# Layer 1 of a two-layer graph attention kernel: ten score products and seven own-slot products as a few wide VectorE instructions

## The chip, the cores and the metric

The kernel runs on one core of one Trainium2 chip. The metric is device time of one execution in microseconds (us). Before the change it is 2040.26 us, the median of three runs (2037.29 to 2045.88).

## What is computed

Two attention layers over a graph of 8192 nodes with 128 features, with a sparse adjacency mask. Both read the same integer matrix `adj` (8192 x 8192, 268 MB), in which a row has nine entries or so. Cut to what matters:

```python
h = jnp.maximum(_layernorm(x, axis=-1), 0.0)
x = x + _L0_gnn_ref(h, adj, W, a)                 # leaky_relu(s1[:, None] + s2[None, :]), masked softmax, elu
h = jnp.maximum(_layernorm(x, axis=-1), 0.0)
# layer 1
q = h @ Wq.T + bq;  k = h @ Wk.T + bk;  v = h @ Wv.T + bv
scores = q @ k.T / sqrt(128)
scores = where(adj > 0, scores, -9e15)
x = x + elu(softmax(scores, axis=-1) @ v)
```

## The kernel before, in words

The nodes are cut into 64 tiles of 128 (one node per partition). Layer 0 (`survey`) streams `adj` from memory once, packs each row into a list of its neighbours, writes node features to a table in memory (`table0`, later `table1`), and does the attention of layer 0 on rows gathered from it. Layer 1 (`attend`) uses the lists again and never reads `adj`. The change is in layer 1 alone.

For each tile of layer 1 the neighbours lie in ten slots of `Gt`: slot 0 is the node itself, slots 1 to 6 are its own first six neighbours (together `OWN` = 7), and slots 7 to 9 (`CHUNKS` = 3) hold 384 rows for nodes with more neighbours, dealt out over the partitions. Each slot is a row of 132 words per partition, of which `DE` = 129 are used (128 features and a one). `Gt` has four such buffers (`GROUP`), taken in turn.

The engines' instructions are written out for all tiles, in the order of `attend`, and each engine works through its own list in order. Tiles are staggered: in step t, DVE works on tile t - 3 (weigh and sum), t - 2 (scores), t (prepare) and t - 4 (finish). What each does:

- **POOL** waits until the `Gt` buffer is free (`summed` of the tile four before, counted up by L882) and then issues nine indirect gathers, L602, one a slot. They take their row numbers from `idx_now` in SBUF. Slot 0 comes by a plain transfer that SP issues at L522.
- **PE** makes the query vector u of a tile (L1530), deals u and the unit matrix to the three chunks (L1515, L1516, counted in `own_done`), scatters the chunk scores back to their nodes (`scatter`, L1382, counted in `scattered`), spreads the row maximum (L1389), and sums the weighted chunk rows (`sum_up`, L1396).
- **DVE**, in order, in one step: `weigh` (L866), `keep_u` (L1114), `score1` (seven times L1120 on the own slots, three times L1124 on the chunks, each a product with a factor and a sum by the accumulator, then `spread_scores`, L839), `add_slot` (L876 once, then L873 six times, each of which adds p times a slot to `acc_sb`), `maxima` (L852, L854, L856, where L854 waits for `scattered`), `total` (L882, L885), `prepare` (L1103 to L1109), `below` (L860, which waits for PE's L1389), `finish` (L891, L894) and `publish` of the next step (L1097).
- **ACT** moves PE's results from PSUM to SBUF (L1306, L1310, L1313) and makes the exponentials (L1198, L1202, L1318, L1319).

Of the kernel before, what the change touches and what calls it, by code (L numbers as in the profile page):

```python
# [41 lines left out]
def two_layer_graph_attention(nc, x, adj, W, a, Wq, bq, Wk, bk, Wv, bv, out):  # L42
# [22 lines left out]
    with ExitStack() as ctx:  # L65
# [145 lines left out]
        prod = place([ROWS, DE])  # L211
        accn = place([2, D])
# [395 lines left out]
        def _(dve):  # L608
# [269 lines left out]

            def total(tt, k, width):
                dve.wait_ge(acc_done, tt + 1)  # L880
                dve.wait_ge(chained, OWN * (tt + 1))
                nc.vector.tensor_tensor(acc_sb[:, k, 0:width], acc_ps[k][:, 0:width], acc_sb[:, k, 0:width], ALU.add)\  # L882
                  .then_inc(summed, 1)
                dve.wait_ge(summed, tt + 1)
                nc.vector.reciprocal(rinv[:, k, :], acc_sb[:, k, width - 1:width]).then_inc(rinv_done, 1)  # L885
# [207 lines left out]
            with dve.Else():  # L1093
# [18 lines left out]
                def keep_u(t, b):  # L1112
                    dve.wait_ge(u_done, t + 1)
                    nc.vector.tensor_tensor(u_row[:, b, P:], u_ps, mix_bias[:, 1, :], ALU.add).then_inc(u_kept, 1)  # L1114

                def score1(u, b, k, n):
                    dve.wait_ge(rows_in[b], 16 * (ROWS - 1) * n)
                    dve.wait_ge(self_in[b], 16 * n)
                    for c in range(OWN):
                        nc.vector.scalar_tensor_tensor(out=prod[:, c, :], in0=Gt[:, b, c, 0:DE], scalar=SCALE, in1=u_row[:, b, P:],  # L1120
                                                       op0=ALU.mult, op1=ALU.mult, accum_out=l10[:, k, c:c + 1])
                    dve.wait_ge(own_done, u + 1)
                    for c in range(CHUNKS):
                        ins = nc.vector.scalar_tensor_tensor(  # L1124
                            out=prod[:, OWN + c, :], in0=Gt[:, b, OWN + c, 0:DE], scalar=SCALE, in1=uq_ps[k][:, c, :],
                            op0=ALU.mult, op1=ALU.mult, accum_out=l10[:, k, OWN + c:OWN + c + 1])
                    ins.then_inc(score_done, 1)
                    spread_scores(T + u, k, b)

                def attend(g):  # L1130
                    for b in range(GROUP):
# [11 lines left out]
                        if live(t, 3):  # L1143
                            for c in range(OWN):
                                add_slot(T + t - 3, m, back, c, DE)
# [10 lines left out]

                publish(0, 0)
# [399 lines left out]
```

## Time and profile before

| | us |
|---|---|
| median of three runs | 2040.26 |
| the profiled execution, its own time | 2041.44 |
| its span, from first to last instruction | 2039.70 |
| busy: PE, DVE, POOL, ACT | 1260.7, 1285.1, 1130.4, 770.2 |
| busy DVE from 1200 to 1400 (layer 1) | 112.57 of 200 |
| busy POOL in the same stretch | 124.69 of 200 |

In layer 1, from about 1125 us on, transfers are light (53 GB/s). Times of a row are counted from the start of the span. DVE's instructions overlap by a little: a row may start up to 0.08 us before the one ahead of it ends, so busy times add up to more than the time that passes. In a row of the timeline the first number is the start, the second the duration (of all instructions that the row merges), and the bracket tells the idle time of the engine before it and what ended it.

### The profile page before, as it was taken

What the parts mean: (1) busy time and instruction counts of PE and PEld (TensorE: products, weight loads), DVE (VectorE), ACT (ScalarE), POOL (GpSimd) and SP (SyncE); (2) the same over time, 40 slices, a digit from 0 to 9 for tenths busy, and PEclk for the clock granted to TensorE, in tenths of its full rate; (3) what the DMA queues carried; (4) which work ended last, traced back from release to release, by engine and by line L of the source; (5) the groups of instructions that cost most, each with busy time, mean ns of one, the idle gap of its engine ahead of it and who ended that gap; (6) DMA issues with size and microseconds to landing.
All of it is one profiled execution on the core that took longest, in us unless ns stands there. A gap on an engine that the chain in (4) does not pass through costs nothing.

```text
span 2039.7 us, 23050 instructions
## 1 busy us (share of the span) xinstructions
PE 1260.7 (62%) x5314; PEld 968.6 (47%) x5362; DVE 1285.1 (63%) x6912; ACT 770.2 (38%) x1507; POOL 1130.4 (55%) x1206
## 2 busy tenths in 40 slices
PE   2756766766776676676653355666666665665566
PEld 1433444444444444444443245555555655555555
DVE  4556777767777777777775255565555565565555
ACT  2865566565656665656621011111111111111111
POOL 1345555555555555555563656666666666666661
PEclk9876777676677766767755566666665566666665
DMA  9788989998899998998621211222221222222121
GB/s 314 288 308 319 324 310 331 318 333 288 321 335 322 322 331 306 334 327 315 239 56 39 57 43 49 53 53 52 55 54 53 54 53 53 54 54 53 47 55 31
DMA packets 122262, 372.40 MB, mean 183 GB/s; under 512 B 34577, under 2 KB 67858, under 8 KB 89362
## 3 DMA queue, kind: packets, MB, share of 16 engines
q1 hardware_dynamic: 75458, 289.83, 38.7%
q0 software_dynamic: 38464, 81.08, 15.3%
q10 hardware_dynamic: 8208, 0.03, 0.2%
q8 instruction: 46, 0.75, 0.1%
q14 instruction: 86, 0.70, 0.1%
HBM read 358.12 MB, written 12.72 MB: 182 GB/s over the span
## 4 chain that ended last, share of the span: by engine, by line
DVE 46%; another core or an unknown queue 25%; PE 11%; issue 9%; ACT 5%; DMA 2%; SPq 1%; POOL 0%; DVEq 0%; ACTq 0%; POOLq 0%
DVE arena L873 8%; PE psum L1389 4%; DVE arena L699 3%; DVE arena L758 3%; ACT arena L1171 3%; DVE arena L761 2%; DVE arena L1120 2%; DVE arena L791 2%; DVE arena L866 2%; DVE arena L891 1%; DMA table<-arena 1%; PE psum L1526 1%; PE psum L1527 1%; DVE arena L1124 1%
## 5 line engine op out<-in xcount | busy, mean ns | idle before, releaser
L572 POOL DMA_INDIRECT arena<-table,arena x576 | 549.1, 953 | 432.9 <-DVE arena L827 269.7
L602 POOL DMA_INDIRECT arena<-table,arena x576 | 553.0, 960 | 335.1 <-DVE arena L882 165.5
L1171 ACT ACTIVATE arena<-arena 128x2048 bf16<-128x2048 int32 x256 | 485.4, 1897 | 26.1 <-DMA arena<-in_adj_dram 26.0
L1349 PE MATMUL psum<-arena 128*128 128x512 bf16 x976 | 331.8, 484 | 114.5 <-ACT arena L1171 59.2
L1396 PE MATMUL psum<-arena 128*128 128x131 f32 (+1 forms) x768 | 207.6, 442 | 302.5 <-DVE arena L866 274.3
L1396 PEld LDWEIGHTS psum<-arena 128*128 128x128 f32 x768 | 172.9, 324 | 317.2 <-issue 316.7
L873 DVE SCALAR_TENSOR_TENSOR arena<-arena 128x131 f32<-128x131 f32 (+1 forms) x768 | 268.5, 350 | 36.8 <-DVE arena L876 15.5
L1349 PEld LDWEIGHTS psum<-arena 128*128 128x128 bf16 x1024 | 116.8, 124 | 286.7 <-issue 177.7
L1306 ACT ACTIVATE arena<-psum 128x384 f32<-128x384 f32 x64 | 31.5, 492 | 493.5 <-remote 456.3
L1389 PEld LDWEIGHTS psum<-arena 128*128 128x128 f32 x768 | 148.2, 273 | 90.5 <-DVE arena L856 63.9
L1389 PE MATMUL psum<-arena 128*128 128x1 f32 x768 | 141.5, 300 | 66.5 <-DVE arena L856 52.4
L854 DVE TENSOR_TENSOR arena<-psum,arena 128x18 f32<-128x18 f32 x128 | 22.1, 173 | 251.4 <-remote 248.9
L1382 PEld LDWEIGHTS psum<-arena 128*128 128x128 f32 x768 | 148.6, 281 | 45.5 <-DVE arena L839 35.7
L1382 PE MATMUL psum<-arena 128*128 128x18 f32 x768 | 141.4, 318 | 42.2 <-DVE arena L839 33.0
L1526 PE MATMUL psum<-arena 128*128 128x128 f32 x128 | 47.6, 471 | 186.6 <-ACT arena L1313 117.1
L1220 ACT ACTIVATE arena<-psum 128x465 f32<-128x465 f32 x64 | 35.7, 558 | 295.5 <-PE psum L1413 135.0
L860 DVE TENSOR_TENSOR arena<-arena,psum 128x3 f32<-128x3 f32 x128 | 19.7, 154 | 181.6 <-remote 98.3
L1413 PE MATMUL psum<-arena 128*128 128x155 f32 x384 | 119.9, 484 | 2.9 <-DVE arena L791 1.4
L1526 PEld LDWEIGHTS psum<-arena 128*128 128x128 f32 x128 | 29.8, 290 | 193.3 <-ACT arena L1313 121.2
L1515 PE MATMUL psum<-arena 128*128 128x128 f32 x384 | 116.7, 405 | 1.0 <-issue 1.0
L1516 PE MATMUL psum<-arena 128*128 128x129 f32 x384 | 112.3, 390 | 0.0
L1120 DVE SCALAR_TENSOR_TENSOR arena<-arena 128x129 f32<-128x129 f32 x448 | 101.0, 288 | 7.8 <-DMA arena<-table,arena 5.3
(199 smaller groups left out, 2230.0 us busy)
## 6 DMA issues: line engine op xcount, KB each, us to landing
arena<-in_adj_dram SPq DMA_DIRECT2D x256, 1024.0 KB
arena<-table,arena POOLq DMA_INDIRECT x1152
table<-arena POOLq DMA_DIRECT2D x32, 132.0 KB, 5.3
arena<-table SPq DMA_DIRECT2D x64, 66.0 KB
table<-arena SPq DMA_DIRECT2D x16, 256.0 KB
arena<-table SPq DMA_DIRECT2D x64, 64.0 KB
out_dram<-arena SPq DMA_DIRECT2D x16, 256.0 KB
arena<-in_x_dram SPq DMA_DIRECT2D x4, 0.5 KB, 12.1
```

What stands on the lines that cost most here:

```text
L572: pool.indirect_dma_start(Gt[:, v % GROUP, c + 1, :], None, table0, bass.IndirectOffsetOnAxis(idx_now[:, v % GROUP, c:c + 1], 0))\
L602: pool.indirect_dma_start(Gt[:, t % GROUP, c + 1, 0:D], None, table1, bass.IndirectOffsetOnAxis(idx_now[:, t % GROUP, c:c + 1], 0))\
L873: nc.vector.scalar_tensor_tensor(out=acc_sb[:, k, 0:width], in0=Gt[:, r, c, 0:width], scalar=p10[:, k, c:c + 1], in1=acc_sb[:, k, 0:width] ...
L1120: nc.vector.scalar_tensor_tensor(out=prod[:, c, :], in0=Gt[:, b, c, 0:DE], scalar=SCALE, in1=u_row[:, b, P:], op0=ALU.mult, op1=ALU.mult, ...
L1171: nc.scalar.activation(mask[:, k, q * QUARTER:(q + 1) * QUARTER], adj_sb[:, k, q, :], ACT.Relu, accum_out=sum_all[:, bass.ds(tile, 1), q:q ...
L1349: nc.tensor.matmul(V[k], shifted[:, s, :], mask[:, k, s * 512:(s + 1) * 512], start=(s == 0), stop=False)
L1382: last = nc.tensor.matmul(by_slot_ps[k], owned[:, r, c, :], slot_e[:, k, c, :], start=(c == 0), stop=(c == CHUNKS - 1))
L1389: last = nc.tensor.matmul(max_ps[k][:, c:c + 1], mine[:, r, c * P:(c + 1) * P], neg_max[:, k, :], start=True, stop=True)
L1396: last = nc.tensor.matmul(acc_ps[k][:, 0:width], weighted[:, c, :], Gt[:, r, OWN + c, 0:width], start=(c == 0), stop=(c == CHUNKS - 1))
L1413: last = nc.tensor.matmul(deal_ps[v % 2][:, c, :], mine[:, v % GROUP, c * P:(c + 1) * P], dealt[:, v % GROUP, :], start=True, stop=True)
L1515: nc.tensor.matmul(own_ps[m][:, c, :], mine_c, ident[:, :], start=True, stop=True)
L1516: last = nc.tensor.matmul(uq_ps[m][:, c, :], mine_c, u_row[:, j, P:], start=True, stop=True)
```

## The change

`score1` makes the ten scores with three instructions: one product of all seven own slots with u (128 x 903), one product of the three chunks with the dealt u in PSUM (128 x 387), and one sum over the last axis of all ten (1290 words in, 10 out). `add_slots` takes the place of seven calls of `add_slot` in layer 1: one product of the seven own slots with p (128 x 903), and one sum over the slots (903 words in, 129 out, read with a step of 129 words). The factor 1/sqrt(128) goes into u: `keep_u` multiplies u and adds a bias that was scaled once before layer 1. Where one of the new instructions reads what one before it wrote, it waits for it by a count (`e_done`, `score_done`, `chained`). The buffers `slots` and `scaled_bias` are new. Layer 0 and all other engines stay as they are.

```diff
+            def add_slots(t, k, r):
+
+                nc.vector.tensor_tensor(slots[:, :, :], Gt[:, r, 0:OWN, 0:DE], cut_k(p10[:, k, 0:OWN], DE), ALU.mult)\
+                  .then_inc(chained, 1)
+                dve.wait_ge(chained, OWN * T + 2 * t + 1)
+                nc.vector.tensor_reduce(acc_sb[:, k, 0:DE], slots.rearrange("p c d -> p d c"), AX.X, ALU.add).then_inc(chained, 1)
...
             def total(tt, k, width):
                 dve.wait_ge(acc_done, tt + 1)
-                dve.wait_ge(chained, OWN * (tt + 1))
+                dve.wait_ge(chained, OWN * (tt + 1) if tt < T else OWN * T + 2 * (tt - T + 1))
...
                 def keep_u(t, b):
                     dve.wait_ge(u_done, t + 1)
-                    nc.vector.tensor_tensor(u_row[:, b, P:], u_ps, mix_bias[:, 1, :], ALU.add).then_inc(u_kept, 1)
+                    nc.vector.scalar_tensor_tensor(out=u_row[:, b, P:], in0=u_ps, scalar=SCALE, in1=scaled_bias[:, :],
+                                                   op0=ALU.mult, op1=ALU.add).then_inc(u_kept, 1)
...
                     dve.wait_ge(self_in[b], 16 * n)
-                    for c in range(OWN):
-                        nc.vector.scalar_tensor_tensor(out=prod[:, c, :], in0=Gt[:, b, c, 0:DE], scalar=SCALE, in1=u_row[:, b, P:],
-                                                       op0=ALU.mult, op1=ALU.mult, accum_out=l10[:, k, c:c + 1])
+                    nc.vector.tensor_tensor(prod[:, 0:OWN, :], Gt[:, b, 0:OWN, 0:DE],
+                                            u_row[:, b:b + 1, P:].to_broadcast([P, OWN, DE]), ALU.mult).then_inc(e_done, 1)
                     dve.wait_ge(own_done, u + 1)
-                    for c in range(CHUNKS):
-                        ins = nc.vector.scalar_tensor_tensor(
-                            out=prod[:, OWN + c, :], in0=Gt[:, b, OWN + c, 0:DE], scalar=SCALE, in1=uq_ps[k][:, c, :],
-                            op0=ALU.mult, op1=ALU.mult, accum_out=l10[:, k, OWN + c:OWN + c + 1])
-                    ins.then_inc(score_done, 1)
+                    nc.vector.tensor_tensor(prod[:, OWN:ROWS, :], Gt[:, b, OWN:ROWS, 0:DE], uq_ps[k], ALU.mult)\
+                      .then_inc(e_done, 1)
+                    dve.wait_ge(e_done, T + 2 * u + 2)
+                    nc.vector.tensor_reduce(l10[:, k, :], prod[:, :, :], AX.X, ALU.add).then_inc(score_done, 1)
...
-                            for c in range(OWN):
-                                add_slot(T + t - 3, m, back, c, DE)
+                            add_slots(t - 3, m, back)
```

On DVE, in the middle of layer 1, one step read so before, from `keep_u` to the wait for `scattered`:

```order
L1114 TENSOR_TENSOR arena<-psum,arena 128x129 [waits u_done]
L1120 SCALAR_TENSOR_TENSOR arena<-arena 128x129 [waits self_in3,rows_in3]
L1120 SCALAR_TENSOR_TENSOR arena<-arena 128x129 x6
L1124 SCALAR_TENSOR_TENSOR arena<-arena,psum 128x129 [waits own_done]
L1124 SCALAR_TENSOR_TENSOR arena<-arena,psum 128x129 x2
L839 TENSOR_TENSOR arena<-arena 128x54 [waits score_done]
L876 TENSOR_SCALAR arena<-arena 128x129
L873 SCALAR_TENSOR_TENSOR arena<-arena 128x129 [waits chained] x6
L852 TENSOR_TENSOR arena<-arena 128x7
L854 TENSOR_TENSOR arena<-psum,arena 128x18 [waits scattered]
```

and the same stretch of the changed kernel, whose line numbers are higher (L841 is L839 of before, L854 and L856 are L852 and L854):

```order
L1123 SCALAR_TENSOR_TENSOR arena<-psum,arena 128x129 [waits u_done]
L1129 TENSOR_TENSOR arena<-arena 128x903 [waits self_in1,rows_in1]
L1132 TENSOR_TENSOR arena<-arena,psum 128x387 [waits own_done]
L1135 TENSOR_REDUCE arena<-arena 128x10 [waits e_done]
L841 TENSOR_TENSOR arena<-arena 128x54 [waits score_done]
L883 TENSOR_TENSOR arena<-arena 128x903
L886 TENSOR_REDUCE arena<-arena 128x129 [waits chained]
L854 TENSOR_TENSOR arena<-arena 128x7
L856 TENSOR_TENSOR arena<-psum,arena 128x18 [waits scattered]
```

Seventeen products (and ten reads of the accumulator, which the list does not show) have become three products and two sums at the same two places; nothing else changed its place.

## Rows read from the trace of the kernel before

**Rows 1.** The page: the chain that ended last, by engine.

```profile
DVE 46%; another core or an unknown queue 25%; PE 11%; issue 9%; ACT 5%; DMA 2%; SPq 1%; POOL 0%; DVEq 0%; ACTq 0%; POOLq 0%
```

**Rows 2.** POOL's timeline, 1509 to 1524 us: start, duration, engine, line, [idle before].

```profile
1509.86 0.96 POOL L602 DMA_INDIRECT arena<-table,arena  x1 [2.82 <-DVE arena L882]
...
1512.42 0.97 POOL L602 DMA_INDIRECT arena<-table,arena  x1 [0.30 <-issue]
1513.69 0.97 POOL L602 DMA_INDIRECT arena<-table,arena  x1 [0.30 <-issue]
...
1519.97 0.94 POOL L602 DMA_INDIRECT arena<-table,arena  x1 [0.30 <-issue]
...
1523.64 0.96 POOL L602 DMA_INDIRECT arena<-table,arena  x1 [2.73 <-DVE arena L882]
```

**Rows 3.** The same stretch on PE and DVE.

```profile
1512.29 0.28 DVE L1120 SCALAR_TENSOR_TENSOR arena<-arena 128x129 f32<-128x129 f32 x1
...
1514.52 0.22 DVE L839 TENSOR_TENSOR arena<-arena 128x54 f32<-128x54 f32 x1
1514.65 0.28 DVE L876 TENSOR_SCALAR arena<-arena 128x129 f32<-128x129 f32 x1
...
1516.06 0.74 PE L1382 MATMUL psum<-arena 128*128 128x18 f32 x6
...
1517.24 0.16 DVE L852 TENSOR_TENSOR arena<-arena 128x7 f32<-128x7 f32 x1
...
1522.78 0.18 DVE L854 TENSOR_TENSOR arena<-psum,arena 128x18 f32<-128x18 f32 x1 [5.38 <-remote]
```

**Rows 4.** Timeline of all engines, another tile, 1237 to 1247 us.

```profile
1238.34 0.28 DVE L1120 SCALAR_TENSOR_TENSOR arena<-arena 128x129 f32<-128x129 f32 x1
...
1238.81 1.06 POOL L602 DMA_INDIRECT arena<-table,arena  x1 [0.30 <-issue]
...
1242.53 0.74 PE L1382 MATMUL psum<-arena 128*128 128x18 f32 x6
...
1243.92 0.94 POOL L602 DMA_INDIRECT arena<-table,arena  x1 [0.30 <-issue]
...
1246.67 0.18 DVE L854 TENSOR_TENSOR arena<-psum,arena 128x18 f32<-128x18 f32 x1 [1.96 <-remote]
```

**Rows 5.** Timeline, two places where L866 runs as a gather starts.

```profile
1334.14 0.55 DVE L866 TENSOR_TENSOR arena<-arena 128x384 f32<-128x384 f32 x1
1334.30 1.21 POOL L602 DMA_INDIRECT arena<-table,arena  x1 [0.30 <-issue]
...
1346.51 0.55 DVE L866 TENSOR_TENSOR arena<-arena 128x384 f32<-128x384 f32 x1
1346.82 1.05 POOL L602 DMA_INDIRECT arena<-table,arena  x1 [0.30 <-issue]
```

**Rows 6.** Groups by line and shape in layer 1: busy us, mean ns, idle before.

```profile
L602 POOL DMA_INDIRECT arena<-table,arena x576 | 553.0, 960 | 335.1 <-DVE arena L882 165.5 <-issue 160.3 <-DMA table<-arena 8.7
...
L1120 DVE SCALAR_TENSOR_TENSOR arena<-arena 128x129 f32<-128x129 f32 x448 | 101.0, 288 | 7.8 <-DMA arena<-table,arena 5.3 <-issue 2.5
L866 DVE TENSOR_TENSOR arena<-arena 128x384 f32<-128x384 f32 x70 | 38.4, 549 | 0.4 <-issue 0.4
L1120 DVE DVE_READ_ACCUMULATOR arena<-arena 128x1 f32 x448 | 35.8, 80 | 1.6 <-issue 1.6
L882 DVE TENSOR_TENSOR arena<-psum,arena 128x129 f32<-128x129 f32 x64 | 18.1, 283 | 0.1
L856 DVE TENSOR_REDUCE arena<-arena 128x1 f32<-128x25 f32 x69 | 12.3, 179 | 2.4
L995 DVE TENSOR_REDUCE arena<-arena 128x64 f32<-128x256 f32 x1 | 0.4, 417 | 0.0
```

**Rows 7.** The chain in order of time, at the start of layer 1.

```profile
1157.47 1.18 issue
...
1169.97 5.55 another core or an unknown queue
```

More of the change, by code:

```diff
@@ L211, in two_layer_graph_attention @@
         prod = place([ROWS, DE])
+        slots = place([OWN, DE])
+        scaled_bias = place([DE])
         accn = place([2, D])
@@ L1155, in attend @@
                             finish(t - 4, T + t - 4, k)
+                nc.vector.tensor_scalar(scaled_bias[:, :], mix_bias[:, 1, :], SCALE, None, ALU.mult).then_inc(dve_consts, 1)
+                dve.wait_ge(dve_consts, DVE_CONSTS + 3)
                 publish(0, 0)
```

## The prediction

> **What bounds the kernel now.** Layer 0 is untouched, so only the stretch from about 1125 us on counts. I read the page's chain first [rows 1]: DVE 46%, and a quarter on releasers that the profile cannot name. That chain names L873 and L1120 among its costliest pieces, which would make DVE's products look worth their length. The timeline of one tile says otherwise.
>
> POOL goes through layer 1 in 64 blocks of nine gathers. One block starts at 1509.86, its last gather at 1519.97 ends at 1520.91, and the next block starts at 1523.64 [rows 2]. So a period of 13.78 us is 11.05 of gathering and 2.73 of waiting. The wait ends with L882, which frees the buffer (60 of the 64 blocks have one like it; together 165.5 us of POOL's idle time [rows 6]). What is L882 behind? It stands on DVE after L854, and L854 waits 5.38 us, until 1522.78, for PE's scatter [rows 3]. The reader should see two things here. DVE is through with its products at 1517.24 and then has nothing to do for over 5 us. And PE's own record of the scatter, L1382, ends at 1516.80, six us before L854 starts.
>
> So what holds L854? I compare a tile in which everything lies otherwise [rows 4]: there the scatter's record ends at 1243.27 and the last gather at 1244.86, and L854 starts at 1246.67. From the scatter's end to L854 the two tiles have 5.98 and 3.40 us. From the last gather's end they have 1.87 and 1.81 us. The release follows the gathers and not DVE or PE. Why a count from PE reaches DVE only then, no row tells; that it does, I take from the two tiles, and by the starts of L854 it holds within about 0.2 us for nearly all blocks. The loop that sets layer 1 is then: nine gathers (11.05), 1.87 to L854, 0.86 over L856 and L882 to the next gather. 11.05 + 1.87 + 0.86 = 13.78. DVE's score and slot work is in none of the three. It matters by what it does to the gathers.
>
> **What it does to the gathers.** An undisturbed gather takes 0.94 us and is followed by 0.30 [rows 2]. At 1334.30 one took 1.21, while L866, a product with both inputs in SBUF, ran from 1334.14 to 1334.69; at 1346.82 one took 1.05, with L866 until 1347.06 [rows 5]. L866 ended 0.39 and 0.24 after these starts; the gathers lost 0.27 and 0.11. Both agree with one rule: a gather that finds such a product running stands still until the product ends, and loses that rest less 0.13 us. The small losses of 0.03 in [rows 2] fit it too, since L1120 ends 0.16 after the gather's start there. Products of 129 words cost so little because one ends every 0.21 us.
>
> The Trainium skill speaks to this on both sides, in "SBUF — State Buffer", Who interferes with whom. It says that an instruction with two SBUF inputs keeps a GpSimd instruction that reads SBUF waiting to its end; by that rule, the trace agrees, to 0.02 us in [rows 5]. It also says that `tensor_tensor` was seen not to stall a DMA's descriptors, which would leave the time where it is; that is rival B below.
>
> **The change on DVE.** Product: 549 ns for 384 words and 283 for 129 [rows 6] are 1.04 ns a word, so 903 words take 1.09 us and 387 words 0.55. Sum: 179 ns for 25 words and 417 for 256 [rows 6] give 1.03 ns a word, so 1290 words take 1.48 and 903 take 1.08. A wait for one's own engine costs some 0.04, and without one the next instruction starts 0.08 before the end.
> - Scores, before: from 1512.29 to L839 at 1514.52, 2.23 us [rows 3]. After: 1.01 + 0.55 + 0.04 + 1.48 + 0.04 = 3.12. That is 0.89 longer.
> - Own slots, before: from 1514.65 to L852 at 1517.24, 2.59 [rows 3]. After: 1.09 + 0.04 + 1.00 = 2.13. That is 0.46 shorter. For the sum over slots that step by 129 words no row has a price; below it is the contiguous 1.08, above I allow twice that.
> - `keep_u` stays one instruction with one input in PSUM: nothing. The scaled bias is once 0.3 us, beside the first gathers.
>
> DVE's work grows by 0.43 us a tile, by 1.5 with the dear sum. The 5.4 us before L854 hide either; in the other pattern 1.96 us [rows 4] do. Without that cover it would be 28 us over 64 tiles. The scatter's input comes 0.9 later, at about 1515.6, and PE turns to it at 1516.06 [rows 3]: hidden as well.
>
> **The change on POOL.** The first score product would start at 1512.29, where L1120 does, and end at 1513.38. The third gather starts at 1512.42, finds it running (L1120, at the same place, was ahead of the gather too) and loses 0.96 - 0.13 = 0.83, against 0.03 now: +0.80. The next gathers then start at 1514.49 and 1515.73. The chunk product has an input in PSUM and the two sums have one input; I take them to cost the gathers nothing, and if the long sum did, the fourth gather would lose 0.7 and the fifth nothing, which is the same total. The slot product starts at 1512.29 + 3.12 + 0.13 = 1515.54, that is 0.19 ahead of the fifth gather, and ends at 1516.63. The fifth gather loses 0.90 - 0.13 = 0.77, against the 0.03 of the fourth now: +0.74. The other gathers meet nothing new. Together +1.54 us a block.
>
> In the other pattern the score product starts at 1238.34 and the gather at 1238.81 [rows 4] would lose 0.62 - 0.13 = 0.49 instead of its 0.12; the slot product would again start 0.2 ahead of a gather and cost 0.77. That is +1.14. I take the first pattern, as a longer block gives PE more time before its end.
>
> **The ends.** At the start of layer 1 POOL gathers four tiles without a pause. There DVE's instructions come singly, with 0.4 to 1.3 us before each, from 1157.47 to 1169.97, and then L839 waits 5.55 more [rows 7]. Three instructions in place of twenty should pass sooner. The most that this gives is until the gathers end at about 1170, some 7 us; the least is nothing. I take 4. The last tiles have no gathers beside them; one tile's scores and slots are on the path, +0.4.
>
> **Sum.** 60 blocks x 1.54 = 92.4, less 4, plus 0.4: +89 us on the profiled execution's 2041.4, thus 2130. That execution is 1.2 us above the median of the runs, so the forecast is 2129 us.
>
> **Rivals.**
> - A, only one product hits. The slot product leads its gather by 0.19 us; where the sum before it takes 0.12 us more than worked out, the gather comes first, and DVE rather than POOL gives way. Then 60 x 0.80 = 48 and the time is 2084. The same mechanism, and half the price.
> - B, no hit: what [rows 5] show is something that a product of 0.55 us does and one of 1.09 does not, or the hold ends early. Then the loop stands as it is, and the present small losses go: 60 x 0.1 us, and up to 7 at the start. 2030 to 2040. Against it is that both rows fit one number.
> - C, faster: the chain of the page is right and DVE sets the period [rows 1]. Then one counts as the busy times do: ten products at 0.288 + 0.080 [rows 6] are 3.68 against 3.12, and the slots 2.59 against 2.13, in all 1.02 a tile, and 64 tiles give 65 us: 1976. It would need DVE to be what L854 waits for. The 5.38 us of idle time there speak against it, and so does that products overlap, so that ten take 2.23 and not 3.68.
> - D, the sum over slots with its step costs twice as much and DVE reaches L854 late. That needs over 5 us in the first pattern. It adds nothing unless the second pattern prevails; then up to 10 us.
>
> **Chances.** Two hits 0.60, one hit 0.22 (A), D on top of either 0.02, no hit 0.10 (B), C 0.06. A change of 0.5% is 10 us, about what a measurement of this kernel can tell from none. Slower is both hits, one hit and D: 0.84. Of B some goes below the 10 us by the gain at the start: same 0.09, and faster 0.07. The range leaves out B and C. It begins under A, at 2076, where the start gives its 7, and ends at 2142, where the start gives nothing and the third gather loses another 0.2 a block: 2076 to 2142. The second pattern throughout (60 x 1.14, 2105) lies inside.
>
> **What would show it.** Right: gathers of about 1.7 us, two in each block, at the start of which a 903-word product runs on DVE; blocks of 12.6 us; a period of 15.3; L854's follower still starting 1.8 to 1.9 after the last gather's end; DVE idle before it by 6 us. Wrong: gathers of 0.95 beside products of 1.09 (B), or a start of that instruction that moves with DVE's sums and not with the last gather (C). If two hits a block are there and the period does not grow, the loop was misread.

## The result, and the profile after

The changed kernel takes 2016.88 us, the median of four runs (2002.33 to 2019.41). The kernel before takes 2038.78 us beside it (2035.83 to 2045.88, four runs). The ratio is 0.9871, with a 95% interval of 0.9825 to 0.9917. The forecast was 2129 us with a range from 2076, so the result is on the other side of no change and outside the range. The profiled execution is the fastest of the four: 2002.33 us, with a span of 2000.6. Against the trace of before it shows a gain of 39.1 us, where the medians have 21.9.

The page's chain, which answers to [rows 1]:

```profile
DVE 50%; another core or an unknown queue 19%; issue 12%; PE 10%; ACT 4%; POOL 2%; DMA 1%; SPq 1%; DVEq 0%; ACTq 0%; POOLq 0%
```

The groups of layer 1 by line and shape (busy us, mean ns | idle before), which answer to [rows 6]. L604 is the gather, L602 of before; L1129 and L1132 are the score products, L1135 their sum; L883 and L886 are the product and the strided sum over the slots:

```profile
L604 POOL DMA_INDIRECT arena<-table,arena x576 | 626.1, 1087 | 238.6 <-issue 171.0 <-DVE arena L891 58.9 <-DMA table<-arena 8.7
L886 DVE TENSOR_REDUCE arena<-arena 128x129 f32<-128x903 f32 x64 | 111.9, 1748 | 2.2
...
L1135 DVE TENSOR_REDUCE arena<-arena 128x10 f32<-128x1290 f32 x64 | 95.8, 1497 | 2.2
L883 DVE TENSOR_TENSOR arena<-arena 128x903 f32<-128x903 f32 x64 | 70.0, 1094 | 0.0
L1129 DVE TENSOR_TENSOR arena<-arena 128x903 f32<-128x903 f32 x64 | 69.7, 1089 | 9.4 <-DMA arena<-table,arena 9.3
```

The first row holds both halves of the story. The gathers' own time grew from 553.0 to 626.1 us, so 73.1 were lost to stalls, where I had forecast 92. But the time in which POOL waited for DVE to free a buffer (L891, L882 of before) fell from 165.5 to 58.9 us, by 106.6, which I had not forecast at all. With 10.7 more between the gathers (171.0 against 160.3) that makes 22.8 us less.

One block of the changed kernel shows the stalls, and why the waits went (timeline of POOL, DVE and PE; L1391 is PE's scatter, L856 the instruction that waits for its count and L854 of before; a train means gathers that follow one another 1.25 us apart):

```profile
1734.27 1.09 DVE L1129 TENSOR_TENSOR arena<-arena 128x903 f32<-128x903 f32 x1
1734.43 1.74 POOL L604 DMA_INDIRECT arena<-table,arena  x1 [0.30 <-issue]
...
1737.39 0.21 DVE L841 TENSOR_TENSOR arena<-arena 128x54 f32<-128x54 f32 x1
1737.52 1.09 DVE L883 TENSOR_TENSOR arena<-arena 128x903 f32<-128x903 f32 x1
1737.73 1.70 POOL L604 DMA_INDIRECT arena<-table,arena  x1 [0.30 <-issue]
...
1738.65 1.77 DVE L886 TENSOR_REDUCE arena<-arena 128x129 f32<-128x903 f32 x1
1738.73 1.31 PE L1391 MATMUL psum<-arena 128*128 128x18 f32 x6
1739.73 0.94 POOL L604 DMA_INDIRECT arena<-table,arena  x1 [0.30 <-issue]
1740.32 0.17 DVE L854 TENSOR_TENSOR arena<-arena 128x7 f32<-128x7 f32 x1
1740.40 0.18 DVE L856 TENSOR_TENSOR arena<-psum,arena 128x18 f32<-128x18 f32 x1
...
1740.98 0.94 POOL L604 DMA_INDIRECT arena<-table,arena  x1 [0.30 <-issue]
```

Two gathers of 1.74 and 1.70 us, each with a 903-word product ahead of it: so far this is the forecast. But L856 starts at 1740.40, 0.36 us after the scatter's end, while POOL goes on with gathers 1.25 apart. In [rows 3] the same instruction started 5.98 us after the scatter's end and not until the gathers were over. Here nothing was held, and no block of this stretch waits for its buffer.

It is not so everywhere. From 1762 to 1789 no long product met a gather, and POOL gathered in one unbroken train:

```profile
1759.94 1.46 PE L1391 MATMUL psum<-arena 128*128 128x18 f32 x6 [0.42 <-issue]
...
1772.01 0.94 POOL L604 DMA_INDIRECT arena<-table,arena  x1 [0.30 <-issue]
1772.36 0.18 DVE L856 TENSOR_TENSOR arena<-psum,arena 128x18 f32<-128x18 f32 x1 [9.63 <-remote]
1773.26 0.94 POOL L604 DMA_INDIRECT arena<-table,arena  x1 [0.30 <-issue]
...
1788.24 0.95 POOL L604 DMA_INDIRECT arena<-table,arena  x1 [0.30 <-issue]
...
1794.16 0.16 DVE L862 TENSOR_TENSOR arena<-arena,psum 128x3 f32<-128x3 f32 x1 [20.04 <-remote]
...
1802.49 0.96 POOL L604 DMA_INDIRECT arena<-table,arena  x1 [13.30 <-DVE arena L891]
```

DVE stood still for 20.04 us, the count came 5.0 us after the last gather's end, and POOL waited 13.30 us for its buffer. The same train shows that the end of a train is not the only place where a count comes through: the scatter ended at 1761.40 (1.46 us from 1759.94), and L856 started 10.96 us later at 1772.36, between two gathers 1.25 us apart. So counts are kept back for 5 to 20 us in a long unbroken train, and where gathers are stalled most of them come at once. DVE's waits give the sum of it. In layer 1 before (us in total, times, longest):

```profile
DVE arena L854 <- remote: 242.1, 60, 5.5
DVE arena L860 <- PE psum L1389: 56.1, 58, 2.4
```

and in layer 1 after:

```profile
DVE arena L856 <- remote: 114.1, 19, 15.8
DVE arena L862 <- remote: 96.7, 13, 20.0
```

The wait for the scatter came 60 times before and 19 times after. There are fewer waits, but longer ones, and some now fall on L862 (L860 of before), which waits for PE to spread the row maximum. Of the gain in the profiled execution, 23.5 us lie between the first and the last gather of layer 1 (879.4 us before, 855.9 after). The rest is that layer 1 began 6.9 us earlier, which no changed instruction explains, and that the tail behind the last gather is 8.8 us shorter, which no run looked into.

### The profile page after: what moved, and what is told of

It is laid out like the page before. It is cut to its first block, busy times and chain, and to the rows that moved or that the text cites. A ratio compares the mean times of both kernels' runs of the same rounds, so it can differ in the third digit from the quotient of the medians.

```text
span 2000.6 us, 21643 instructions
## 1 busy us (share of the span) xinstructions
PE 1256.1 (63%) x5314; PEld 974.4 (49%) x5362; DVE 1361.0 (68%) x5505; ACT 772.2 (39%) x1507; POOL 1204.1 (60%) x1206
## 4 chain that ended last, share of the span: by engine, by line
DVE 50%; another core or an unknown queue 19%; issue 12%; PE 10%; ACT 4%; POOL 2%; DMA 1%; SPq 1%; DVEq 0%; ACTq 0%; POOLq 0%
DVE arena L875 5%; DVE arena L701 3%; DVE arena L760 3%; DVE arena L763 3%; DVE arena L886 3%; ACT arena L1180 3%; DVE arena L1135 2%; POOL arena L604 2%; DVE arena L793 2%; DVE arena L868 2%; DVE arena L883 2%; DVE arena L1129 2%; PE psum L1398 1%; PE psum L1405 1%
## 5 line engine op out<-in xcount | busy, mean ns | idle before, releaser
L574 POOL DMA_INDIRECT arena<-table,arena x576 | 549.7, 954 | 424.1 <-DVE arena L829 262.2
L604 POOL DMA_INDIRECT arena<-table,arena x576 | 626.1, 1087 | 238.6 <-issue 171.0
L1405 PEld LDWEIGHTS psum<-arena 128*128 128x128 f32 x768 | 172.0, 322 | 414.0 <-issue 413.5
L862 DVE TENSOR_TENSOR arena<-arena,psum 128x3 f32<-128x3 f32 x128 | 19.6, 153 | 260.6 <-remote 196.0
L1391 PEld LDWEIGHTS psum<-arena 128*128 128x128 f32 x768 | 161.6, 303 | 28.4 <-issue 15.6
L1391 PE MATMUL psum<-arena 128*128 128x18 f32 x768 | 152.7, 334 | 25.7 <-issue 14.2
L1398 PEld LDWEIGHTS psum<-arena 128*128 128x128 f32 x768 | 143.6, 264 | 50.5 <-issue 26.6
L1398 PE MATMUL psum<-arena 128*128 128x1 f32 x768 | 132.8, 288 | 32.1 <-issue 16.9
L875 DVE SCALAR_TENSOR_TENSOR arena<-arena 128x131 f32<-128x131 f32 x384 | 130.6, 340 | 6.5 <-DVE arena L878 2.0
L1211 ACT ACTIVATE arena<-arena 128x3 f32<-128x3 f32 x128 | 26.2, 205 | 273.5 <-DVE arena L862 160.5
L1525 PE MATMUL psum<-arena 128*128 128x129 f32 x384 | 117.5, 406 | 0.0
L886 DVE TENSOR_REDUCE arena<-arena 128x129 f32<-128x903 f32 x64 | 111.9, 1748 | 2.2
L856 DVE TENSOR_TENSOR arena<-psum,arena 128x18 f32<-128x18 f32 x128 | 21.9, 171 | 124.8 <-remote 122.6
```

Of the source, the lines that this page charges most:

```text
L574: pool.indirect_dma_start(Gt[:, v % GROUP, c + 1, :], None, table0, bass.IndirectOffsetOnAxis(idx_now[:, v % GROUP, c:c + 1], 0))\
L604: pool.indirect_dma_start(Gt[:, t % GROUP, c + 1, 0:D], None, table1, bass.IndirectOffsetOnAxis(idx_now[:, t % GROUP, c:c + 1], 0))\
L875: nc.vector.scalar_tensor_tensor(out=acc_sb[:, k, 0:width], in0=Gt[:, r, c, 0:width], scalar=p10[:, k, c:c + 1], in1=acc_sb[:, k, 0:width] ...
L886: nc.vector.tensor_reduce(acc_sb[:, k, 0:DE], slots.rearrange("p c d -> p d c"), AX.X, ALU.add).then_inc(chained, 1)
L1391: last = nc.tensor.matmul(by_slot_ps[k], owned[:, r, c, :], slot_e[:, k, c, :], start=(c == 0), stop=(c == CHUNKS - 1))
L1398: last = nc.tensor.matmul(max_ps[k][:, c:c + 1], mine[:, r, c * P:(c + 1) * P], neg_max[:, k, :], start=True, stop=True)
```

## The experiments

My theory after the result had two parts: the long products cost the gathers 73 us, and the pauses that they force on POOL break its trains and let the counts through (theory H in the first two sets of expectations, S in the later ones). The main rival was that DVE's work itself gained: fewer instructions, no reads of the accumulator, shorter chains (R, later W). Each comparison below was made on one chip, with the kernel before run beside the others, and ratios are only taken within one: in the first and the fourth comparison, for which the same chip number is on record, the kernel before took 2013.27 and 2037.5 us.

### First comparison: pauses without the change, the change without most of its stalls, and its halves

Before: 2013.27 us (2006.08 to 2022.9, 19 runs).

**pause** is the kernel before with two memsets of 0.78 us on POOL in each block:

```diff
+        idle = place([800])
...
+                        if c in (2, 4):
+                            nth = 2 * t + (2, 4).index(c)
+                            at_least(pool, idle_done, nth)
+                            nc.gpsimd.memset(idle[:, :], 0.0).then_inc(idle_done, 1)
```

> Theory H (runs of gathers): PE's counts, the scatter's among them, are held back while POOL issues gather on gather at 1.25 us without a break, and come through when the run is broken; in the changed kernel the wide products break it. So in the kernel before, with nothing changed on DVE and two idle memsets of 800 words on POOL in each block of layer 1 (after the third and the fifth gather, an estimated 0.7 to 0.9 us each), L854 should start before the last gather ends, and 1960 to 2015 us come out although POOL has 1.6 us more to do a block. Theory R (DVE's work): the gain of the change is that DVE has fewer instructions and counts; pauses on POOL then only lengthen the loop by 60 x 1.6 = 96 us, about 2135 us, with L854 still 1.85 us after the last gather.

Measured: 1988.16 us, ratio 0.987 (0.9845 to 0.9894). Two memsets that compute nothing give what the whole change gave, with DVE's program untouched. POOL's wait for the buffer was 35.5 us in 16 pieces. The counts were not all let through: DVE still waited 41 times for the scatter in layer 1, 139.6 us in all, where the trace of before has 242.1.

**split** is the changed kernel with its two 903-word products cut into seven of 129 words, so that no gather meets one long product:

```diff
-                nc.vector.tensor_tensor(slots[:, :, :], Gt[:, r, 0:OWN, 0:DE], cut_k(p10[:, k, 0:OWN], DE), ALU.mult)\
-                  .then_inc(chained, 1)
+                for c in range(OWN):
+                    ins = nc.vector.tensor_tensor(slots[:, c, :], Gt[:, r, c, 0:DE], p10[:, k, c:c + 1].to_broadcast([P, DE]),
+                                                  ALU.mult)
+                ins.then_inc(chained, 1)
...
-                    nc.vector.tensor_tensor(prod[:, 0:OWN, :], Gt[:, b, 0:OWN, 0:DE],
-                                            u_row[:, b:b + 1, P:].to_broadcast([P, OWN, DE]), ALU.mult).then_inc(e_done, 1)
+                    for c in range(OWN):
+                        ins = nc.vector.tensor_tensor(prod[:, c, :], Gt[:, b, c, 0:DE], u_row[:, b, P:], ALU.mult)
+                    ins.then_inc(e_done, 1)
```

> The changed kernel with each product of 903 words made as seven products of 129 words; the sums stay. No product then runs longer than 0.28 us, so gathers stay at 0.95 us. Theory H: runs are unbroken again, the wait for the scatter ends 1.85 us after the block's last gather, period 13.8 us, 2025 to 2045 us. Theory R: DVE still has no chained additions and no reads of the accumulator, so the gain stays: 2000 to 2020 us.

Measured: 2041.64 us, ratio 1.015 (1.0108 to 1.0192). The gathers' mean was 984 ns, between the 960 of before and the 1087 of the changed kernel: most of the stall was gone, though 25 gathers still took over 1.3 us, 18 of them beside the seven short score products. POOL's wait for the buffer was 150.7 us in 37 pieces. Taking most of the stalls away made the kernel slower.

**scores_only** makes the change in `score1` alone (the three new instructions at L1129 to L1135 and the factor in u), and **slots_only** the one in `add_slots` alone:

```diff
-                            for c in range(OWN):
-                                add_slot(T + t - 3, m, back, c, DE)
+                            add_slots(t - 3, m, back)
```

> Only the scores are changed, the own slots are added one by one as before. One wide product a block, so one gather of about 1.7 us. Theory H: the run is broken once, after the third gather, and six gathers follow unbroken; most blocks still end held, with 0.8 us more, 2040 to 2085 us, or, if one break is enough, 1990 to 2020. Theory R: DVE's work grows by 0.9 us a tile, nothing is gained: 2040 or slower. This run tells mostly how many breaks are needed.

> Only the own slots are changed. One wide product a block, at about the fifth gather (1.7 us). Theory H: the run is broken in its middle, four gathers on either side, so the counts come through in many blocks: 1980 to 2020 us. Theory R: seven chained instructions less; it would carry the gain of 20 us or more too: at or below 2015 us. H wants a long gather in the blocks whose wait for the scatter ends early, R does not.

Measured: scores_only 2004.44 us, ratio 0.9954 (0.9925 to 0.9984); slots_only 2017.3 us, ratio 1.0023 (0.9998 to 1.0048). Each has half of the stalls (gather means of 1011 and 1007 ns) and keeps more of the waits: 98.2 us in 30 pieces and 121.4 us in 41, against 58.9 in 14 with both. The two ratios multiply to 0.998 and both together gave 0.987 on the chip of the result, so the gain is not a sum of the parts' own costs. That fits trains that have to be broken twice, but the 0.998 and the 0.987 are from different comparisons.

These expectations were given in us, for a kernel before of 2038.78 us. As ratios to that, the one for pause held, but split was to come out at 0.993 to 1.003 and slots_only at 0.971 to 0.991, and both were slower than that; scores_only fell between its two cases. That split is slower than the kernel before, and not equal to it, no run explains.

### Second comparison: a chip on which no count is held

Before: 1715.1 us (1714.36 to 1719.25, 7 runs), 15 to 16% less than in the other comparisons, for the same kernel. **before_again** is that kernel unchanged and **after_again** the changed one. **pause_end** has both memsets behind the ninth gather of a block, and **pace3** has three, after the second, the fourth and the sixth:

```diff
+                    for n in range(2):
+                        at_least(pool, idle_done, 2 * t + n)
+                        nc.gpsimd.memset(idle[:, :], 0.0).then_inc(idle_done, 1)
```

```diff
+                        if c in (1, 3, 5):
+                            nth = 3 * t + (1, 3, 5).index(c)
+                            at_least(pool, idle_done, nth)
+                            nc.gpsimd.memset(idle[:, :], 0.0).then_inc(idle_done, 1)
```

> The kernel before, for its trace beside the others. If layer 0 alone is what differs between the two comparisons, POOL's layer 1, from its first to its last gather, takes 879 us here too and begins near 1105 us instead of 1125. If the blocks run otherwise, some waits of POOL for L882 are missing and layer 1 is shorter.

> The changed kernel once more, beside the experiments, since the kernel before ran at 2013 us in the last comparison and at 2039 in the first. Theory H: the change gains what its stalls give back and loses what they cost, so against 2013 it lies between split (1.015 of before) and pause (0.987): 1990 to 2015 us. Theory R (less work on DVE): the ratio of the first comparison, 0.987.

> The kernel before with the same two memsets of 800 words on POOL, but both after the ninth gather, so that the run of nine stays unbroken. Theory H: the counts come through 1.85 us after the run as before, POOL would have waited 2.7 us there anyway and spends 1.7 of them on the memsets: the same as before, 2005 to 2025 us. If what helped in pause was only that POOL has more to do a block, and not that the run is broken, this one would come out at 1988 too.

> The kernel before with three memsets of 800 words in a block, after the second, fourth and sixth gather. Each adds 0.64 us (the two of pause did), so nine gathers take 13.1 us, 1.45 a gather. In the start of layer 1 of the kernel before, DVE's instructions came one by one every 1.4 us while gathers ran at 1.25. If a gather takes 1.4 us of whatever holds the counts, then here nothing is left over from gather to gather: hardly any wait for L888 by POOL, and layer 1 takes 64 x 13.1 = 840 us and the whole 1975 to 1990. If one long break is what counts and not the mean rate, it is pause plus 0.64 x 60: 2010 to 2030.

Measured: before_again 1715.47 us; after_again 1769.88 us, ratio 1.0309 (1.0291 to 1.0327); pause_end 1808.67 us, ratio 1.0543 (1.0525 to 1.056); pace3 1834.73 us, ratio 1.0691 (1.067 to 1.0713). Here the change is slower, by 3%. The expectations for after_again, pause_end and pace3 were written for a chip that holds the counts, and all three missed. The kernel before on this chip, its gathers, its scatter and its DVE waits of layer 1:

```profile
L602 POOL DMA_INDIRECT arena<-table,arena x576 | 555.5, 964 | 184.0 <-issue 175.2 <-DMA table<-arena 8.7
```

```profile
1400.02 0.84 PE L1382 MATMUL psum<-arena 128*128 128x18 f32 x6 [1.25 <-DVE arena L839]
...
1401.85 0.94 POOL L602 DMA_INDIRECT arena<-table,arena  x1 [0.30 <-issue]
1402.67 0.17 DVE L854 TENSOR_TENSOR arena<-psum,arena 128x18 f32<-128x18 f32 x1
...
1403.10 0.94 POOL L602 DMA_INDIRECT arena<-table,arena  x1 [0.30 <-issue]
```

```profile
DVE arena L1120 <- DMA arena<-table,arena: 194.3, 64, 5.7
DVE arena L860 <- PE psum L1389: 13.0, 47, 1.1
```

POOL never waits for a buffer. L854 starts with no idle time in the middle of an unbroken train. What DVE waits for is the gathered data, and its waits for the row maximum are 1.1 us at most. POOL alone sets layer 1, so whatever lengthens its work is paid in full. The changed kernel's rows beside it:

```profile
L604 POOL DMA_INDIRECT arena<-table,arena x576 | 612.8, 1064 | 184.0 <-issue 175.2 <-DMA table<-arena 8.8
```

```profile
1407.24 1.10 DVE L1129 TENSOR_TENSOR arena<-arena 128x903 f32<-128x903 f32 x1 [3.10 <-DMA arena<-table,arena]
1407.67 1.49 POOL L604 DMA_INDIRECT arena<-table,arena  x1 [0.30 <-issue]
```

The gathers take 612.8 - 555.5 = 57.3 us more and nothing else on POOL changes; the spans differ by 1771.9 - 1713.7 = 58.2. That is the mechanism of the forecast with no relief to set against it. The pauses are paid likewise. Three of 0.64 us in 64 blocks are 123 us, and pace3 took 119.6 more.

### Third comparison: all four on one chip

Before: 2032.59 us (2027.46 to 2037.92, 17 runs), a chip that holds the counts. The kernels are those above under new labels.

> The changed kernel with both 903-word products cut into seven of 129. The two chips so far differ: on the first, counts from PE stay away while gathers follow one another without a break (before 2013 us), on the second they never do (before 1715 us). Theory S (stalled gathers are the change's cost, broken runs its gain): with short products no gather is stalled for long, so on a chip of the second kind, where POOL alone sets layer 1, the time is that of before within 0.3% (gather mean about 0.97 us), and not the 1.031 of the changed kernel. On a chip of the first kind it is 1.00 to 1.02, as there (1.015), since the runs are whole again. Rival W (the changed kernel's time comes from its wider DVE work and from the strided sum, whatever the gathers do): split keeps the sums and has more DVE time than the changed kernel, so it would be as slow as that or slower on a chip of the second kind, 1.03 or more.

> The changed kernel beside the others on one chip. Theory S: 0.985 to 0.99 where the kernel before takes 2010 us or more, 1.03 where it takes about 1715 us. Rival N (the second chip's sign was a matter of that one comparison): the ratio does not go with the time of the kernel before.

> The kernel before with a POOL memset of 0.78 us (0.64 us of pitch) after the third and the fifth gather of each block; DVE as before. Theory S: on a chip of the first kind 0.985 to 0.99; on one of the second kind every pause is paid, 64 x 2 x 0.64 = 82 us to 96 us, a ratio of 1.05. Rival W: no gain on any chip that is not DVE's.

> The same two memsets, both behind the ninth gather, so that a block of nine is whole and 1.3 to 1.5 us separate it from the next. On a chip of the second kind 1.054, as measured there. On a chip of the first kind theory S in its strong form (it is the break within a block that lets PE's scatter count through) says no gain: the wait of 2.7 us before the next block now starts 1.4 us later, so half of the pause is hidden in it, and the time is that of before to 3% more, clearly above the pauses within the block. Rival P (any time that POOL spends off the gathers helps alike): the same 0.987 as pauses within the block.

Measured: split_c 2077.96 us, ratio 1.0207 (1.0184 to 1.023); after_c 2013.8 us, 0.9921 (0.9896 to 0.9945); pause_c 2012.37 us, 0.9911 (0.9889 to 0.9933); pause_end_c 2030.45 us, 1.0002 (0.9986 to 1.0017). POOL's waits for the buffer were 189.3 us in 37 pieces with split_c, 54.2 in 14 with after_c, 54.5 in 22 with pause_c and 67.9 in 57 with pause_end_c. A pause inside the block gains, and the same pause at its end does not. Where the two differ is seen in one block each. Of pause_c (L1388 is the scatter, L860 waits for it, and L888 frees the buffer):

```profile
1517.72 0.74 PE L1388 MATMUL psum<-arena 128*128 128x18 f32 x6
1517.85 1.05 POOL L604 DMA_INDIRECT arena<-table,arena  x1 [0.30 <-issue]
...
1518.86 0.17 DVE L860 TENSOR_TENSOR arena<-psum,arena 128x18 f32<-128x18 f32 x1
...
1519.16 0.28 DVE L888 TENSOR_TENSOR arena<-psum,arena 128x129 f32<-128x129 f32 x1
1519.21 0.95 POOL L604 DMA_INDIRECT arena<-table,arena  x1 [0.30 <-issue]
```

Of pause_end_c (L1387 is the scatter, L859 what waits for it):

```profile
1510.63 0.90 PE L1387 MATMUL psum<-arena 128*128 128x18 f32 x6
...
1513.85 0.94 POOL L604 DMA_INDIRECT arena<-table,arena  x1 [0.30 <-issue]
1514.79 1.60 POOL L609 MEMSET arena<- 128x800 f32 x2
1516.65 0.18 DVE L859 TENSOR_TENSOR arena<-psum,arena 128x18 f32<-128x18 f32 x1 [5.37 <-remote]
...
1517.52 0.97 POOL L604 DMA_INDIRECT arena<-table,arena  x1 [1.12 <-DVE arena L887]
```

In the first, L860 starts 0.40 and L888 0.70 after the scatter's end with the gathers still going. In the second the count comes 1.86 us after the last gather's end, 5.12 after the scatter's, much as in [rows 3], although POOL is at its memsets meanwhile. So what holds the count is the gathers and not a busy POOL, and the memsets vanish in a wait that was there anyway (1.12 us where it was 2.73). In pause_c about half of the blocks are like the one shown, in pause_end_c nearly all. Over layer 1, DVE waited for the scatter, in pause_c and then in pause_end_c:

```profile
DVE arena L860 <- remote: 113.7, 31, 7.1
DVE arena L859 <- remote: 322.8, 59, 9.1
```

Against the expectations, after_c and pause_c gained a little less than 0.985 to 0.99, split_c lies at the upper end of 1.00 to 1.02, and pause_end_c is as theory S had it.

### Fourth comparison: is it the breaks or DVE's work, and how many breaks?

Before: 2037.5 us (2029.62 to 2044.57, 13 runs). **split_pause** is split with the memsets of pause, **pause_one** the kernel before with one memset, after the fourth gather (`if c in (3,)`), and **pace3_c** is pace3.

> The split kernel (1.015 and 1.021 of before in two comparisons on chips of the first kind) with POOL pauses of 0.64 us after the third and the fifth gather. If whole runs of gathers are what costs split its time (S), the pauses free it as they free the kernel before: 0.985 to 0.995 of before. If the time of split lies in DVE's extra work and the strided sum (W), the pauses add to it or leave it: 1.015 or more. On a chip of the second kind the pauses are simply paid: 1.05.

> The kernel before with one POOL pause of 0.64 us, after the fourth gather. On a chip of the first kind: if one break ahead of the fifth gather is enough for PE's scatter count, half the cost of two pauses is saved and the ratio is about 0.98; if the count of the scatter needs a break of its own later in the block, the time is between that of before and that with two pauses, 0.99 to 1.00. On the second kind 1.025 (64 x 0.64 us = 41).

> The kernel before with three pauses, after the second, fourth and sixth gather; longest unbroken run then three and the next block's two. On a chip of the first kind: no count is held, POOL's block is 11.05 + 3 x 0.64 = 13.0 us plus 0.3 and follows the last at once: 64 x 13.3 = 850 us for layer 1, which is what two pauses gave (848.6), so 0.985 to 0.995. Fewer holds can't pay more than the pauses cost. On the second kind 1.069, as measured there.

Measured: split_pause 2008.06 us, ratio 0.9873 (0.9832 to 0.9915); pause_one 2046.05 us, ratio 1.005 (1.0027 to 1.0072); pace3_c 1994.68 us, ratio 0.9804 (0.9766 to 0.9843). POOL's waits for the buffer, in this order (pace3_c had none of this kind; its POOL waited for issue alone):

```profile
POOL arena L606 <- DVE arena L899: 22.5, 9, 3.2
```

```profile
POOL arena L604 <- DVE arena L888: 131.8, 30, 5.8
```

```profile
POOL arena L604 <- issue: 147.1, 573, 0.3
```

and DVE's longest waits of pace3_c in layer 1, beside which its waits for the scatter are 1.8 us in all (L866 is L860 of before, and L1395 spreads the row maximum):

```profile
DVE arena L1126 <- DMA arena<-table,arena: 270.9, 63, 7.1
DVE arena L866 <- PE psum L1395: 16.3, 28, 1.2
```

split_pause has all of split's DVE work, the strided sum included, and goes from 1.5 to 2% slower than before to 1.3% faster by two memsets. DVE's work by itself is thus neither the gain nor the loss. pause_one missed both of its forecasts on such a chip (0.98, or 0.99 to 1.00): one break a block leaves 30 waits of 4.4 us in the mean, where the trace of before has 58 of 2.9 [rows 6]. There DVE waits less for the scatter (L860) than for the row maximum (L866) and for a count of its own (L845, L839 of before), which came late as well:

```profile
DVE arena L866 <- remote: 156.1, 28, 8.2
DVE arena L845 <- remote: 83.7, 26, 4.7
DVE arena L860 <- remote: 42.0, 18, 8.1
```

pace3_c came out better than its forecast of 0.985 to 0.995. It has the lowest ratio of all runs on such a chip, and is clearly slower than before (1.069) on the other kind.

## Why the prediction was wrong

**The step that failed is in "What bounds the kernel now": that L854's release follows the last gather's end, 1.87 us after it, whatever the gathers do.** From it came the loop 11.05 + 1.87 + 0.86, in which longer gathers can only lengthen the period. The number was right for a train of nine gathers 1.25 us apart, and pause_end_c repeats it at 1.86. But it was a property of that train. Where a train is broken, L856 starts 0.36 us after the scatter (1740.40), and the block's 1.87 + 0.86 are no longer there at all; so POOL's waits for a buffer fell from 165.5 to 58.9 us, and two pauses that break the train give the same 0.987 without the change. The two tiles of [rows 3, 4] could not tell "after the last gather" from "once a train lets up", since in both the last gather is where the train lets up. [rows 7] could have warned me: the waits there are of another length (the count for L839 came at 1175.5, some 6 us after the last gather of a train of 36, not 1.87), so the delay is longer behind a longer train. What L839 waits for there is moreover a count of DVE's own (`score_done`), so it was never a matter of PE alone. I read them as a start-up matter and priced them at 4 us.

Point by point:

- **The stall rule** held. In the block above L1129 ends 0.93 after the gather's start, which gives a loss of 0.80, and the gather took 1.74 instead of 0.94; L883 gives 0.75 and the gather took 1.70. So 73.1 us were lost against 92.4 forecast, with 109 gathers over 1.3 us where I counted 120. By the Trainium skill ("SBUF — State Buffer", Who interferes with whom) an instruction with two SBUF inputs blocks a GpSimd read to its end, and the trace agrees for these products. The remark in the same section of the Trainium skill that `tensor_tensor` did not stall a DMA's descriptors does not carry over to these indirect gathers, which read their indices from SBUF. The sums and the product with an input in PSUM cost the gathers nothing, as I took it: the gathers that start beside them take 0.94 us in the median (61 beside L1135, 59 beside L886, 7 beside L1132). Short products can do the same when they follow one another without a break: in split a gather that started at 1272.54, among the seven score products (1272.08 to 1273.58), took 1.86 us, which is the same rule counted to the end of the last of them (1.04 less 0.13).
- **DVE, scores**: from L1129's start to L841's is 3.12 us (1734.27 to 1737.39), exactly the sum.
- **DVE, slots**: mis-sized. The sum over slots with its step took 1748 ns; I took 1083, with a bound of twice that. So from the slot product to L854 it is 2.80 (1737.52 to 1740.32), not 2.13. The Trainium skill ("Advanced Engine Details and Errata", Memory Cachelines) says that accesses which each fall on another 16-byte line pay a penalty; the row agrees and comes to 1.6 times what I took for words in a row. It was hidden, as rival D said it would be: split_pause carries it and is fast.
- **The period** did not grow, though two hits a block are there: from the first to the last gather a tile takes 13.4 us in the mean (855.9 / 64), and 13.7 before. That is the case the prediction named as "the loop was misread".
- **The range** ends at 2142, where the terms named for that end (2129, 4 for the start, 60 x 0.2) come to 2145. Nothing hangs on it, since the result lies 59 us below the other end.
- **Rival C**, the only fast one, gave 1976 through DVE as the bound. It falls with pause, which gains with DVE's work as it was, and with split_pause, which gains with more instructions on DVE than the changed kernel has. The list lacked the rival that came true: that a stalled gather breaks the train which holds the count. Its price stood in [rows 6]: up to the 165.5 us of waits, against 92 of stalls.
- **The sign goes with the comparison.** In the second one the forecast's mechanism is all that is seen and the change costs 3.1%. In the two others in which it was timed it gains 1.3 and 0.8%. That it is the chip that makes the difference is argued: the fast kind was met in one comparison only.

## What to carry to other kernels

When a wait ends a fixed time after something, ask what else ends there too, and find or make a case in which the two come apart before adding that time into a loop; here a pause at the block's end and one in its middle would have done it. A stall on an engine whose work holds another's counts can pay for itself, so price what it releases as well; a kernel whose time rests on such an interplay should be timed on more than one chip, since the same edit was 1.3% faster in one comparison and 3.1% slower in another.

## What the runs showed of the hardware

- **Counts are held while POOL issues indirect gathers 1.25 us apart, on some chips.** On the chips of the result and of the first, third and fourth comparison those from PE come late in such a train, by 5.98 us in [rows 3] and by up to 20 us in the changed kernel. ACT's waits show it too: in pause_end_c L1311 waited 6.85 us with the same releaser. DVE's own counts can be late too (L845 in pause_one, 83.7 us; L839 in [rows 7], 5.55), and in the stretch of [rows 7] even DVE instructions that wait for nothing ran singly, 0.4 to 1.3 us apart. On the chip of the second comparison the kernel that is the same word for word has no wait named "remote" in layer 1 on DVE.
- **The profiler's own records are lost where counts are held.** The trace of before holds 13,728 records of semaphore updates and that of before_again 33,238, for the same program. All traces divide so: 12,700 to 14,500 on the holding chips, 33,000 to 33,500 on the other. So whatever is short there touches the recording too. Every execution on record carries the profiler's figures, and no run tells whether its recording takes part in the holds or only suffers from them. That is the rival that this document leaves open, and it would bear on how much the effect means for a kernel that runs without a profiler. The releasers named in the rows of the holding chips also rest on what is left of these records.
- **That chip is also faster in layer 0.** From 400 to 800 us the kernel before moves 384 GB/s there (last number) and 319 on the other:

```profile
400.00:800.00 400.00, 301.41 (x1306) 186.65 (x1328) 353.63 (x1914) 297.67 (x455) 264.66 (x279) 0.77 1.01 384
```

```profile
400.00:800.00 400.00, 274.51 (x1080) 178.88 (x1099) 294.59 (x1591) 247.27 (x373) 222.00 (x234) 0.69 0.90 319
```

- **What the holds rest on stays open.** From the first to the last gather after_c, split_pause and pace3_c take 854.5, 853.7 and 854.8 us, the changed kernel 855.9 and pause 848.6, though they spend it quite differently; the other chip does the kernel before in 730.7. It looks like a floor of about 1.48 us a gather, as if each gather occupied something for that long, and that was my guess. But pace3_c is no witness for it: its POOL never waits, and the chip without holds takes 853.3 for the same kernel (pace3), so this time is its gathers and pauses and nothing else. A plain queue of that kind, worked out from the gathers' starts, did not tell well which counts were held, and no run looked at the something itself. What it is, why one chip is free of it, and why one break a block was worse than none, no run shows.
- **A `tensor_reduce` of 903 words read with a step of 129 words took 1748 ns**; 1290 words in a row took 1497.
